# Where a wait for the features stands, key tiles by halves, turned shifts one tile later, and zero-filled bias operands in a two-layer graph network

## The reference

```python
def gat_layer(x, W, a_src, a_dst, bias, src, dst, heads, out_c, concat):
    h = (x @ W).reshape(n, heads, out_c)
    e = leaky_relu(einsum(h, a_src)[src] + einsum(h, a_dst)[dst], 0.2)
    ex = exp(e - segment_max(e, dst)[dst])
    alpha = ex / (segment_sum(ex, dst)[dst] + 1e-16)
    return segment_sum(h[src] * alpha, dst) + bias      # 8 heads side by side, or 1
def L0_mix(x):                       # linear attention, 12 heads of 64
    q, k, v = x @ W_qkv.T;  q, k = elu(q) + 1, elu(k) + 1
    kv = einsum("nd,nm->md", k, v);  z = 1 / (q . k.sum(0) + 1e-6)
    return (einsum("nd,md,n->nm", q, kv, z)) @ W_proj.T + b_proj
def L0_ffn(xs):                      # 8 experts, the best 2 of each token
    topv, topi = top_k(softmax(xs @ Wg), 2);  cw = topv / topv.sum(-1)
    return sum_k cw[k] * (relu(xs @ W1[e_k] + b1[e_k]) @ W2[e_k] + b2[e_k])
edge_index = stack([src, dst])       # 40000 edges, sorted by dst, among 1250 nodes
xn = layernorm(x)                    # x: 1250 x 768
x = x + (elu of GAT 8 x 96, then GAT 1 x 768)(xn, edge_index) + L0_mix(xn)
x = x + L0_ffn(layernorm(x))
xn = layernorm(x)
x = x + L1_gnn(xn, edge_index, edge_weight) + L1_mix(xn)   # adapter, 2 GCN; vector mix
x = x + L1_ffn(layernorm(x))         # 2 layers of B-splines, 768 -> 256 -> 768
```

## Time and profile before

| | us |
|---|---|
| median of the three runs | 2888.5 |
| lowest, highest | 2885.83, 2891.29 |
| the profiled execution, its own time | 2892.15 |
| its span in the trace | 2890.4 |
| PE busy in it | 2711.8 |
| mean granted clock of PE | 0.965 |

### The profile page before, as it was taken

One profiled execution on the slowest core, in us unless ns is written; L12 is line 12 of the kernel. 1 busy time (PEld: TensorE's weight loads), 2 busy tenths in 40 slices (PEclk: granted clock), 3 DMA queues, 4 the chain that ended last, 5 costly groups with the idle time before them and its releaser, 6 DMA issues.

```text
span 2890.4 us, 31058 instructions
## 1 busy us (share of the span) xinstructions
PE 2711.8 (94%) x11845; PEld 1880.7 (65%) x11845; DVE 1488.6 (52%) x2300; ACT 978.9 (34%) x1590; POOL 98.6 (3%) x141
## 2 busy tenths in 40 slices
PE   5999999999989899899968999999799999899999
PEld 4786655688866556577745865566577776455555
DVE  6997899499963455521133210243676776422330
ACT  7895110387741132212222201031544442312210
POOL 1000000000000001100030000000000000000000
PEclk9999999999999899789988999999899999999999
DMA  9904221211030301389967110000200001100000
GB/s 239 322 0 90 98 58 69 70 53 52 21 70 6 92 3 52 110 311 360 360 192 153 40 33 33 1 15 1 88 30 30 29 30 66 71 11 6 11 11 11
DMA packets 131740, 238.12 MB, mean 82 GB/s; under 512 B 18639, under 2 KB 99572, under 8 KB 131118
## 3 DMA queue, kind: packets, MB, share of 16 engines
q1 hardware_dynamic: 116418, 192.97, 21.9%
q0 software_dynamic: 15200, 43.44, 4.5%
HBM read 173.10 MB, written 63.25 MB: 82 GB/s over the span
## 4 chain that ended last, share of the span: by engine, by line
PE 81%; DVE 11%; DMA 3%; issue 2%; ACT 2%; DVEq 1%; SPq 0%; POOL 0%; ACTq 0%; POOLq 0%
PE ps L927 23%; PE ps L1316 14%; PE ps L1300 14%; PE ps L1127 4%; PE ps L881 4%; PE ps L1175 4%; PE ps L1186 4%; PE ps L944 3%; DVE arena L1912 3%; DVE arena L1913 2%; DMA arena<-in_x_dram 2%; PE ps L1239 2%; PE ps L1037 1%; PE ps L1228 1%; PE ps L1156 1%
## 5 line engine op out<-in xcount | busy, mean ns | idle before, releaser
L927 PE MATMUL ps<-arena 128*125 128x384 f32 x2160 | 716.4, 492 | 11.0 <-issue 6.1
L927 PEld LDWEIGHTS ps<-arena 128*125 128x125 f32 x2160 | 407.2, 190 | 297.1 <-issue 21.8
L1316 PE MATMUL ps<-arena 128*125 128x384 f32 x1280 | 414.6, 487 | 14.4 <-DVE arena L2324 14.4
L1300 PE MATMUL ps<-arena 128*128 128x312 f32 (+1 forms) x1536 | 407.4, 428 | 15.0 <-DVE arena L2324 15.0
L1300 PEld LDWEIGHTS ps<-arena 128*128 128x128 f32 x1536 | 292.3, 190 | 129.9 <-issue 17.0
L1316 PEld LDWEIGHTS ps<-arena 128*125 128x125 f32 x1280 | 241.0, 188 | 187.8 <-issue 16.2
L2324 DVE SCALAR_TENSOR_TENSOR arena<-arena 128x1250 f32<-128x1250 f32 (+1 forms) x170 | 231.3, 1382 | 114.7 <-PE ps L1300 111.1
L1328 ACT ACTIVATE arena<-ps 128x750 f32<-128x750 f32 (+5 forms) x140 | 108.2, 777 | 504.7 <-PE ps L927 207.8
L881 PE MATMUL ps<-arena 128*125 128x380 bf16 x1280 | 213.1, 328 | 19.1 <-DVE arena L1737 19.1
L881 PEld LDWEIGHTS ps<-arena 128*125 128x125 bf16 x1280 | 173.0, 137 | 59.0 <-issue 14.9
L1847 DVE SCALAR_TENSOR_TENSOR arena<-ps,arena 125x768 f32<-125x768 f32 x30 | 28.7, 955 | 353.7 <-PE ps L1316 292.0
(11 more groups left out here) (313 smaller groups left out, 2638.8 us busy)
## 6 DMA issues: line engine op xcount, KB each, us to landing
arena<-in_L_ffn_W_dram SPq DMA_DIRECT2D x54, 1152.0 KB, 7.6
xs_rows<-arena SPq DMA_DIRECT2D x1, 30720.0 KB, 99.4
arena<-in_kw_dram SPq DMA_DIRECT2D x24, 512.0 KB, 4.6
arena<-al_dst POOLq DMA_DIRECT2D x18, 625.0 KB, 5.0
arena<-xs_rows SPq DMA_DIRECT2D x27, 384.0 KB, 7.1
y_rows<-arena POOLq DMA_DIRECT2D x27, 384.0 KB, 6.7
arena<-in_kw_dram SPq DMA_DIRECT2D x6, 1536.0 KB, 9.8
arena<-in_x_dram SPq DMA_DIRECT2D x2, 3600.0 KB
```

The costliest lines, as they stand in the source:

```text
L927: mm = pe.matmul(slot(g)[0:TILE, 512 * half:512 * half + HALF], xt[:, k, i * TILE:i * TILE + TILE], w[:, k, :], start=(k == 0), stop=(k == ...
L1300: mm = pe.matmul(slot(g)[:, 512 * b:512 * b + wd_], w[:, r % 2, ORDER[p], o * P:o * P + P], feat[place(f)][:, lo + b * wd_:lo + b * wd_ + ...
L1316: mm = pe.matmul(slot(g)[0:TILE, 512 * b:512 * b + HALF], fv[:, q, :], w2c[m][q][:, b * HALF:b * HALF + HALF], start=(p == 0 and q == 0), ...
```

## The change

Four places are changed; what is computed stays the same.

1. DVE's wait for the event `x` (both parts of the features loaded) stands ahead of the edges' `If` before; now it stands inside, ahead of `statistics`, behind `add_block` of the last block but one, and at the start of the `Else`.
2. The key product `mk` takes tiles 0 to 7 as before. Tiles 8 and 9 take their two slots together, and PE computes half 0 of 8, half 0 of 9, half 1 of 8, half 1 of 9. After the second of these it raises `mk_half`, and SP's `send` of piece 5 waits for that event in place of the last `mk` packet.
3. `SHIFTED = 3`: the turned shifts `gT 2` come behind h2 3 in the plan, on PE and on ACT; they were behind h2 2.
4. `cwT` and `b2m` have all 128 rows. When h2 is done and `E_in` has reached its end (ACT's last exponential), POOL fills both with zeros, between its fills and its selects, and then a one-column buffer `csum0`, which raises `choice_zero`; SP loads the 8 rows of `b2m` behind that. ACT writes the first 8 rows of `cwT`. The bias products contract over 128 rows, of which 120 are zeros in both operands.

```diff
--- before.py
+++ after.py
@@ -60,6 +60,7 @@
 
 AHEAD = 4
 QUERIES = 2 * KT
+SHIFTED = 3
 
 
 def query_at(m):
@@ -153,7 +154,7 @@
     packet("alT", 2)
     for i in range(NT):
         packet("h2", i)
-        if i == 2:
+        if i == SHIFTED:
             packet("gT", 2)
     used(a, b)
     for j in range(NT):
@@ -389,6 +390,7 @@
         rsum = rcut(NT)[0:TILE]
         rmax = rcut(NT)[0:TILE]
         csum = rcut(NT)[0:TILE]
+        csum0 = rcut(1)
         slotf = rcut(2 * NT)[0:TILE].rearrange("p (k t) -> p k t", k=2)
         sloti = rcut(2 * NT)[0:TILE].bitcast(I32).rearrange("p (k t) -> p k t", k=2)
         yslotf = rcut(2 * NT)[0:TILE].rearrange("p (k t) -> p k t", k=2)
@@ -413,8 +415,8 @@
         eidi = rcut(NTAU).bitcast(I32)
         rowf = rcut(NTAU)
         rowi = rcut(NTAU).bitcast(I32)
-        cwT = rcut(NODES)[0:EXP]
-        b2m = rcut(D)[0:EXP]
+        cwT = rcut(NODES)
+        b2m = rcut(D)
         assert ro[0] <= 4700
         xf = ct_r[0:TILE, 0:NT * D].rearrange("p (t d) -> p t d", t=NT)
         xfT = [aa_r[:, 750 * n:750 * n + 750].rearrange("p (k n) -> p k n", k=KT) for n in range(2)]
@@ -581,7 +583,10 @@
             def send(key):
                 n = pieces[key]
                 if n >= 3:
-                    sp.wait_ge(packet_ready, last[order[n - 3]] + 1)
+                    if order[n - 3] == ("mWk", 0):
+                        sp.wait_ge(ev("mk_half"), 1)
+                    else:
+                        sp.wait_ge(packet_ready, last[order[n - 3]] + 1)
                 name = key[0]
                 if name in WT:
                     t, lo = WT[name]
@@ -628,7 +633,8 @@
             sp.wait_ge(packet_ready, packets["h2", NT - 1] + 1)
             sp.wait_ge(ev("E_in"), (HEADS + 1) * NT)
             load(wg, A["L0_ffn_Wg"].rearrange("(k p) e -> p k e", p=P), "wg")
-            load(b2m, A["L0_ffn_b2"], "b2m")
+            sp.wait_ge(ev("choice_zero"), 1)
+            load(b2m[0:EXP], A["L0_ffn_b2"], "b2m")
             sp.wait_ge(packet_ready, packets["agg2", NT - 1] + 1)
 
             def expert(t):
@@ -805,12 +811,17 @@
             own.step(pool.iota(taus, [[1, NTAU]], base=0, channel_multiplier=0,
                                allow_small_or_imprecise_dtypes=True))
             own.step(pool.memset(past[:, :, 0:1], 1.0))
+            pool.wait_ge(packet_ready, packets["h2", NT - 1] + 1)
+            pool.wait_ge(ev("E_in"), (HEADS + 1) * NT)
+            own.step(pool.memset(cwT, 0.0))
+            own.step(pool.memset(b2m, 0.0))
             own.settle()
             own.step(pool.affine_select(out=before, in_=before, compare_op=ALU.is_gt, fill=0.0, base=0,
                                         pattern=[[1, P]], channel_multiplier=-1))
             own.step(pool.affine_select(out=under, in_=under, compare_op=ALU.is_gt, fill=0.0, base=0,
                                         pattern=[[1, EXP], [-1, EXP]], channel_multiplier=0))
             own.settle()
+            pool.memset(csum0, 0.0).then_inc(ev("choice_zero"), 1)
             pool.affine_select(out=upto, in_=upto, compare_op=ALU.is_ge, fill=0.0, base=0,
                                pattern=[[1, EXP], [-1, EXP]], channel_multiplier=0).then_inc(ev("tables"), 1)
 
@@ -982,7 +993,21 @@
                         mm = pe.transpose(o16[:, i * 126:i * 126 + TILE],
                                           CT[:, 4 * q + i, j * TILE:j * TILE + TILE], ident16[0:TILE, 0:TILE])
                     ready(mm)
-            token_major("mk", xT, ("mWk", 0), ("mWk", 1))
+            a, b = weights("mWk", 0), weights("mWk", 1)
+            for i in range(NT - 2):
+                token_tile("mk", i, xT, a, b)
+            pair = [take_slot("mk", i) for i in (NT - 2, NT - 1)]
+            for half, w in enumerate((a, b)):
+                w = w.rearrange("p (k n) -> p k n", k=KT)
+                for g, i in zip(pair, (NT - 2, NT - 1)):
+                    for k in range(KT):
+                        mm = pe.matmul(slot(g)[0:TILE, 512 * half:512 * half + HALF],
+                                       xT[:, k, i * TILE:i * TILE + TILE], w[:, k, :],
+                                       start=(k == 0), stop=(k == KT - 1))
+                    if half == 1:
+                        ready(mm)
+                if half == 0:
+                    mm.then_inc(ev("mk_half"), 1)
 
             def products(i, g):
                 emptied(pe, "mv", i)
@@ -1521,8 +1546,8 @@
 
             for q in range(2):
                 g = take(act, "cwT", q)
-                own.step(act.activation(cwT[:, 5 * q * TILE:5 * q * TILE + 3 * TILE], slot(g)[0:EXP, 0:3 * TILE], ACT.Copy))
-                leave(g, cwT[:, (5 * q + 3) * TILE:(5 * q + 5) * TILE], slot(g)[0:EXP, 512:512 + 2 * TILE])
+                own.step(act.activation(cwT[0:EXP, 5 * q * TILE:5 * q * TILE + 3 * TILE], slot(g)[0:EXP, 0:3 * TILE], ACT.Copy))
+                leave(g, cwT[0:EXP, (5 * q + 3) * TILE:(5 * q + 5) * TILE], slot(g)[0:EXP, 512:512 + 2 * TILE])
             turned(0)
             act.wait_ge(ev("b1t"), 1)
             for t in range(NTAU):
@@ -1776,7 +1801,6 @@
                 return norms[0]
 
             dve.wait_ge(ev("cleared"), 1)
-            dve.wait_ge(ev("x"), 32)
             steps = own.n
             with dve.If(flag == 0):
                 for b in range(4):
@@ -1792,11 +1816,13 @@
                         spotted(s % 2, lambda u: spot_of[:, bass.ds(b * SPREAD + u, 1)])
                 dve.wait_ge(ev("tiles_done"), (NB - 1) * SPREAD + CREDIT)
                 add_block((NB - 2) % 4, NB - 2)
+                dve.wait_ge(ev("x"), 32)
                 counted = [statistics(0, acc), statistics(1, acc)]
                 dve.wait_ge(ev("tiles_done"), NB * SPREAD + CREDIT)
                 add_block((NB - 1) % 4, NB - 1)
             own.n, norms[0] = steps, 0
             with dve.Else():
+                dve.wait_ge(ev("x"), 32)
                 counted = [statistics(0, acc), statistics(1, acc)]
                 with dve.Fori(0, NB // 4) as bp:
                     for s in range(4):
```

## The result

The changed kernel takes **2860.93 us** (median of four runs, 2857.45 to 2863.98); the kernel before took 2889.64 beside it. The ratio is 0.9901, with a 95% interval of 0.9889 to 0.9913: 28.7 us less. Forecast were 2859.3 and 29.2 us less.

What follows compares the result with a forecast made beforehand. TensorE, busy 2711.8 of 2890.4 us, was taken as the bound, so edits count by its holes, late feeds or clock. Terms -8.4 - 8.6 - 7.7 + 9.5 - 14.0 = -29.2 gave 2859.3 us, range 2848 to 2875.

Steps and rivals of the forecast that it cites:

- Edit 1, -8.4: Start of the edge loop: DVE's first product starts 9.1 us earlier without the wait for x, 8.4 us is left.
- The step from 9.1 to 8.4: Edge loop: bulk zero copy into xs_rows slows matmuls from 0.162 to 0.176 us each, its end fixed, leaving 8.4 of 9.1.
- Edit 2, -8.6: After the key tiles: PE's 5.95 us hole waiting for piece 5 and 2.63 us of low clock go.
- Edit 3, -7.7: Ahead of the turned shifts: one 7.74 us tile fills PE's 11.1 us hole, 3.4 us of it stay.
- Edit 4, +9.5 ahead of agg2: Before agg2: POOL's fills and a select held by DVE delay `tables` by 9.0 us, plus 0.5 for the clock.
- one of the cases named: POOL's selects before agg2: if the first slips in between two DVE instructions, the second or third is held.
- The rival that POOL isn't held: Before agg2: selects pass before DVE's long operation, `tables` comes about 0.4 us late, total 2850.2 us; chance 8%.
- Edit 4, -14.0 in the bias products: Bias products: filled rows raise the clock; first group takes 9.1 us, second 6.6, instead of 13.16 each; 14.0 us gained.
- one of the two things named as late next: After the bias products: the first rows of xs, said to land within a microsecond of their new use.
- the rival that the stage holds it down: Bias products: low clock belongs to the stage, not the rows, so no rise; total 2873.3 us; chance 12%.
- Slower by paced experts: Expert stage: weight loads lack room and pace the tiles, giving back 35 us, total 2894 us; chance 3%.
- The sum: Whole kernel: -8.4 - 8.6 - 7.7 + 9.5 - 14.0 = -29.2 us, giving 2859.3 us; chance 67%.

Runs made afterwards that it cites:

- the undone edit's medians: Changed kernel with DVE's wait for x back ahead of the edge loop's `If`, other three edits kept: 2867.35 us, ratio 0.9925.
- the undone run: Changed kernel with the key tiles all whole and piece 5 waiting for the last key packet: 2867.93 us, ratio 0.9921.
- the last experiment: Changed kernel with POOL's selects and `tables` event ahead of the fills, plus SHIFTED = 4: 2852.41 us, ratio 0.9873.
- the cut addition: Changed kernel with each of DVE's long bias additions cut into ten of one tile each, POOL's order kept: 2856.42 us in one run.
- undo_zeros: Changed kernel with `cwT` and `b2m` of 8 rows again, no fills and no event for them: 2865.97 us, ratio 0.9916.
- rows32: Changed kernel with POOL's selects ahead of the fills, bias products contracting over 32 rows instead of 128: 2859.82 us, one run.
- rows64: Changed kernel with POOL's selects ahead of the fills, bias products contracting over 64 rows instead of 128: 2868.29 us, one run.
- the run with ones: Changed kernel with POOL's selects ahead of the fills, `b2m` filled with ones instead of zeros: 2846.53 us, one run.

## Why the prediction was right, point by point

- **Edit 1, -8.4:** 9.1 by the table of places ("the ledger" below), 6.4 by the undone edit's medians. The start at 23.6 was 23.7. The step from 9.1 to 8.4, a share lost to the bulk copy, is wrong, as the timelines of SP before and after show:

```profile
35.41 0.66 SPq L550 DMA_DIRECT2D xs_rows<-arena  x1
```

```profile
35.82 0.66 SPq L552 DMA_DIRECT2D xs_rows<-arena  x1
```

The copy is only issued at 35.4 and 35.8 us, after the loop's start in both kernels (32.70 and 23.70), and takes 99.4 and 99.6 us, so the 9 us that were won lie ahead of it and lose nothing to it. In the eleven traces that have the edit PE comes to the first turned tile behind the loop at 245.22 to 247.26 (median 246.60), against 255.88 and 255.89 in the two without it: 9.3 us earlier in the middle. What is lost comes behind the loop: the first token tile takes 10.31 to 11.01 us with the edit and 9.39 and 9.57 without it, because the clock rises later. At that tile's end 8.3 us are left in the middle of the eleven, so that the term was right by two errors that cancel, and that is luck. Why the clock rises later there is open.
- **Edit 2, -8.6:** 8.6 in the ledger, 7.0 by the medians. The two parts of it, 5.95 of hole and 2.63 of clock, are the step as told; the second varies (1.92 in the undone run).
- **Edit 3, -7.7:** 8.5 in the ledger, 7.4 by the medians, a hole of 3.9 left where 3.4 was said. The 0.8 beyond the tile's 7.7 is mostly clock: 48.15 in place of 48.75 us for six tiles. The prediction miscounts by one what follows the turn, five tiles in place of six; it is six (144 records) in place of seven (168), and the 48.75 us are the first six of those seven. The difference, one tile, isn't touched. The 5.39 us taken for the spread was a price from another transfer. The spread's two copies, issued at 965.7 and 966.3 in the changed kernel, land within 5.8 us, so by 972.1 and just ahead of ScalarE's first exponential at 972.88, which waits for h2 4 and not for them; in the last experiment a copy took 8.04.
- **Edit 4, +9.5 ahead of agg2:** 8.9 and 1.0, together 9.9. The fills ended 1.8 us after they began, where the prediction has 2.2 and its own terms, 1.16 and 0.7, give 1.9; the hold swallows the difference. Of the three selects it was the second that was held, one of the cases named. The rival that POOL isn't held has fallen, and the cut addition shows why.
- **Edit 4, -14.0 in the bias products:** 14.7. The first group took 8.29 where 9.1 was said and the second 6.73 where 6.6 was. The first expert rows were late by 0.58 us, one of the two things named as late next. The clock does rise with added rows, from 96 on in these runs, and the rival that the stage holds it down has fallen in undo_zeros and in rows32 and rows64. The Trainium skill, "TensorE: Matmul & The Clock Gate", section "Part 1: The HAM clock gate", makes it a matter of how busy TensorE has been; these runs differ from that, at 12.80 busy of 13.00 us the clock stayed at 0.50 with 64 rows, and the measurement decides.
- **Slower by paced experts:** no. 366 GB/s, PE busy 119.94 of 120.
- **The sum:** -29.2 against -28.7 by the medians, and -32.5 by the two profiled executions. Of the 3.3 us that these show beyond the sum, 2.0 arose between the value tiles and the shifts, where nothing was changed. The clock's rises differ there, as the timelines of PE before and after show:

```profile
858.45 10.81 PE L927 MATMUL ps<-arena 128*125 128x384 f32 x24 [3.13 <-DVE arena L1847]
```

```profile
840.42 9.41 PE L938 MATMUL ps<-arena 128*125 128x384 f32 x24 [2.56 <-DVE arena L1873]
```

Behind that tile PE is 19.42 us earlier, 1.8 more than at the value tiles, and that is most of the 2.0. Two further differences of the traces nearly cancel in the chain that leads over the last scores to DVE's maxima and to the turn of the shifts: the scores take 4.95 and 3.11 us for 24 records, again by the clock, and two copies of the turned scores through memory 11.97 + 7.88 = 19.85 us before and 12.34 + 9.13 = 21.47 after.

## What to carry to other kernels

Read the granted clock of a stretch next to its busy share: where a busy TensorE stays at the lower level, look at how many rows its products contract over, and filling them up with zeros may pay even though it adds nothing to the result. When work is put on a quiet engine, look at what stands behind it on that engine and who waits for that; here 1.9 us of fills placed ahead of three small selects cost 9.9, and placed behind them nothing. When work starts earlier, look at whether the traffic that is said to slow it runs in the time that is won. A wait that stands at the head of a loop or a transfer that waits for the end of a stage should be placed by its first use and its last use, and the next thing that lands late tells how far such a move pays.

## What the runs showed of the hardware that was not expected

Between 64 rows (13.16 and 13.16 us, granted clock 0.50 throughout) and 96 rows (10.00 and 6.73) the granted clock changes altogether, with PE busy nearly all of the time in both (one trace each). Ones in place of zeros in the added rows of one operand gave 8.41 against 8.35. And GpSimd gets its turn at the end of DVE's instruction even where DVE has no gap at all: 0.99 and 0.81 us for two selects beside nine back-to-back additions, 8.19 us for one beside a single addition of nearly the same work. A hole of 2.84 us ahead of agg2 brought the clock to 0.50 in the kernel before (1042 to 1044 us) and left it at 1.00 in the run with ones (1012.2 to 1018), so what such a hole costs differs from one execution to the next.
